# A bias row brought in by two transfers instead of a product, and two steps of a prologue in another order

## What is computed

```python
adj = dep_type_matrix != 0
dep_emb = dep_emb_table[dep_type_matrix]
hi_t = (h @ W1_w[:HID])[:, :, None, :] + dep_emb @ W1_w[HID:] + W1_b
hj_t = (h @ W2_w[:HID])[:, None, :, :] + dep_emb @ W2_w[HID:] + W2_b
relevance = jnp.sum(hi_t * hj_t, axis=-1)
A = jax.nn.softmax(jnp.where(adj, relevance, NEG), axis=2)
h_syn = jax.nn.relu((A @ h) @ gcn_w + gcn_b)
x = _layernorm(x + h_syn @ Wo_w + Wo_b)
```

## Time and profile before

| | us |
|---|---|
| median of 3 runs | 379.76 (379.12 to 379.9) |
| the profiled execution | 380.05 |
| its span, first to last instruction | 378.0 |
| TensorE busy | 372.1 (98%) |
| VectorE, ScalarE, GpSimd busy | 220.7, 142.1, 153.3 |

### The profile page before, as it was taken

One profiled execution on the slowest core, in us unless ns is written; L12 is line 12 of the kernel. 1 busy time (PEld: TensorE's weight loads), 2 busy tenths in 40 slices (PEclk: granted clock), 3 DMA queues, 4 the chain that ended last, 5 costly groups with the idle time before them and its releaser, 6 DMA issues.

```text
span 378.0 us, 10088 instructions
## 1 busy us (share of the span) xinstructions
PE 372.1 (98%) x4011; PEld 340.0 (90%) x4011; DVE 220.7 (58%) x584; ACT 142.1 (38%) x342; POOL 153.3 (41%) x133
## 2 busy tenths in 40 slices
PE   9999999999999999999999999999999999999994
PEld 4789898999989899998989989898998989999994
DVE  2546264674646567464666646476664646756596
ACT  1725442514334252333415234351423425142433
POOL 1333454270815418072450807236080632608035
PEclk9999999999999999999999999999999999999998
DMA  7922023508052260805317071441706245170105
GB/s 228 332 96 85 21 81 81 185 10 255 5 180 84 45 219 5 232 27 164 99 32 231 0 210 53 131 133 19 245 0 192 72 103 161 20 247 2 43 2 211
DMA packets 34851, 42.88 MB, mean 113 GB/s; under 512 B 10128, under 2 KB 29072, under 8 KB 34832
## 3 DMA queue, kind: packets, MB, share of 16 engines
q1 hardware_dynamic: 33600, 41.13, 36.3%
q10 hardware_dynamic: 1232, 1.49, 1.2%
HBM read 30.03 MB, written 12.58 MB: 113 GB/s over the span
## 4 chain that ended last, share of the span: by engine, by line
PE 98%; DVE 0%; POOL 0%; issue 0%
PE banks L447 18%; PE banks L449 18%; PE banks L448 18%; PE banks L547 9%; PE banks L548 9%; PE banks L553 9%; PE banks L526 7%; PE banks L471 7%; PE banks L571 2%; PE banks L560 1%; PE banks L506 1%; PE banks L581 0%; PE banks L597 0%; PE banks L592 0%; DVE xt_sb L1052 0%; PE banks L540 0%
## 5 line engine op out<-in xcount | busy, mean ns | idle before, releaser
L1160 POOL TENSOR_TENSOR x_sb<-x_sb,wob_sb 128x1536 f32<-128x1536 f32 x15 | 52.8, 3519 | 174.8 <-DVE weights L989 163.0
L958 DVE SCALAR_TENSOR_TENSOR hs_lo<-banks,hs_hi 128x256 fp32r<-128x256 f32 x90 | 32.6, 418 | 67.3 <-ACT hs_hi L818 67.2
L447 PE MATMUL banks<-gcn_hi,xt_hi 128*128 128x386 f32 x192 | 66.7, 347 | 0.0
L448 PE MATMUL banks<-gcn_lo,xt_hi 128*128 128x386 f32 x192 | 64.8, 338 | 0.0
L449 PE MATMUL banks<-gcn_hi,xt_lo 128*128 128x386 f32 x192 | 64.8, 337 | 0.0
L547 PE MATMUL banks<-wo_hi,hs_hi 128*128 128x384 f32 x180 | 60.9, 338 | 0.0
L553 PE MATMUL banks<-wo_hi,hs_lo 128*128 128x384 f32 x180 | 60.5, 336 | 0.0
L548 PE MATMUL banks<-wo_lo,hs_hi 128*128 128x384 f32 x180 | 60.5, 336 | 0.0
L759 ACT ACTIVATE gt_sb<-banks,r_sb 128x512 f32<-128x512 f32 x48 | 33.1, 689 | 70.2 <-PE banks L449 70.1
L447 PE MATMUL banks<-xt_hi,m_hi 128*128 128x512 f32 x144 | 57.4, 398 | 0.0
L449 PE MATMUL banks<-xt_hi,m_lo 128*128 128x512 f32 x144 | 56.8, 394 | 0.0
(11 more groups left out here) (101 smaller groups left out, 513.9 us busy)
## 6 DMA issues: line engine op xcount, KB each, us to landing
xt_sb<-in_x_t_dram SPq DMA_DIRECT2D x15, 768.0 KB, 4.6
x_sb<-in_x_dram SPq DMA_DIRECT2D x15, 768.0 KB, 5.6
out_dram<-y_sb SPq DMA_DIRECT2D x30, 384.0 KB, 5.8
adj_sb<-in_adj_dram SPq DMA_DIRECT2D x32, 64.0 KB, 2.3
xt_sb<-in_x_t_dram SPq DMA_DIRECT2D x2, 384.0 KB, 8.4
xt_sb<-in_x_dram SPq DMA_DIRECT2D x1, 768.0 KB, 4.9
w1t_sb<-in_w_t_dram ACTq DMA_DIRECT2D x3, 192.0 KB, 5.6
w2t_sb<-in_w_t_dram SPq DMA_DIRECT2D x3, 192.0 KB, 3.4
```

Source lines behind the costliest of these rows:

```text
L447: pe.matmul(acc, a_hi, b_hi, start=first, stop=False)
L448: pe.matmul(acc, a_hi, b_lo, start=False, stop=False)
L1160: pool.tensor_tensor(x_home(g, slot), x_home(g, slot), wob_sb[:].rearrange("p (o n) -> p o n", o=1).to_broadcast([P, PAIRS, HID]), ALU.add ...
```

## The change

The product of ones and `gb_diag` is gone, and with it `gb_diag`, its three VectorE instructions and the copy of `GB_BANK`. Instead ScalarE's queue writes gcn_b's three columns as one line of 384 numbers into device memory (`gb_line`), issued behind the biases and ahead of `w1t_sb[:, 1]`; behind gcn_w, ScalarE waits until that line has landed and issues a second transfer that repeats it in all 128 partitions of `gb_row`. On TensorE the third product of M's step 0 now stands behind the c products, and c2's share (L603, now L601) behind step 1 of M instead of ahead of it; step 1 waits for the first c2 result.

```diff
-        gb_diag = sb("gb_diag", [P, HID])
+        gb_line = nc.dram_tensor("gb_line", [1, HID], F32).ap()
...
-            def m_stage(c):
+            def m_stage(c, blocks=range(C)):
...
-                for d in range(C):
+                for d in blocks:
...
-            m_stage(0)
+            m_stage(0, range(C - 1))
...
             mm.then_inc(c_mm, 1)
-            pe.wait_ge(ones_ready, 1)
-            pe.wait_ge(gb_diag_ready, 1)
-            pe.matmul(GB_BANK[:, 0:HID], ones[:].to_broadcast([P, P]), gb_diag[:],
-                      start=True, stop=True).then_inc(gb_mm, 1)
+            m_stage(0, range(C - 1, C))
+            pe.wait_ge(c2_ready, 1)
+            m_stage(1)
             pe.wait_ge(c2_ready, 2)
...
-            m_stage(1)
             m_stage(2)
...
+            pe.wait_ge(ones_ready, 1)
...
-            pe.wait_ge(gb_row_ready, 1)
...
             act.dma_start(bias_sb[:], biases).then_inc(bias_loaded, 16)
+            act.dma_start(gb_line.rearrange("o (c p) -> o c p", p=P),
+                          biases[:, 2 * C:3 * C].rearrange("p (o c) -> o c p", o=1),
+                          allow_slow_non_contiguous=True).then_inc(gb_line_loaded, 16)
             for c in range(1, C):
                 act.dma_start(w1t_sb[:, c], w1_t[c * P:(c + 1) * P]).then_inc(w12_loaded[c], 16)
             for c in range(C):
                 act.dma_start(gcn_sb[:, c], gcn_w[c * P:(c + 1) * P]).then_inc(gcn_loaded[c], 16)
+            act.wait_ge(gb_line_loaded, 16)
+            act.dma_start(gb_row[:, 0:HID], gb_line.to_broadcast([P, HID])).then_inc(gb_row_spread, 16)
...
-                    dve.wait_ge(gb_row_ready, 1)
+                    dve.wait_ge(gb_row_spread, 16)
+                    dve.wait_ge(gb_end_zero, 1)
...
-            dve.memset(gb_row[:, HID:HID + 1], 0.0)
-            dve.wait_ge(ident_ready, 1)
-            for c in range(C):
-                a = dve.tensor_scalar(gb_diag[:, c * P:(c + 1) * P], ident[:], gb_sb[:, c:c + 1], None, ALU.mult)
-            a.then_inc(gb_diag_ready, 1)
+            dve.memset(gb_row[:, HID:HID + 1], 0.0).then_inc(gb_end_zero, 1)
...
-            dve.wait_ge(gb_mm, 1)
-            dve.tensor_copy(gb_row[:, 0:HID], GB_BANK[:, 0:HID]).then_inc(gb_row_ready, 1)
```

More of the change, by code:

```diff
@@ L176, in gnn_layernorm_kernel @@
         C_BANK = bank[3], bank[4]
-        GB_BANK = bank[2]
         ROWMAX_BANK = bank[4]
@@ L211, in gnn_layernorm_kernel @@
         c_mm = sem("c_mm")
-        gb_diag_ready = sem("gb_diag_ready")
-        gb_mm = sem("gb_mm")
-        gb_row_ready = sem("gb_row_ready")
+        gb_line_loaded = sem("gb_line_loaded")
+        gb_row_spread = sem("gb_row_spread")
+        gb_end_zero = sem("gb_end_zero")
         c12_sb_ready = sem("c12_sb_ready")
```

## The result

The changed kernel takes **399.45 us** in the median of 5 runs (397.07 to 400.79), before 379.76 (379.12 to 379.94 in 5 runs): a ratio of 1.052, with an interval of 1.048 to 1.056. It is 19.7 us slower. I had predicted 380.0, with a range to 384.6.

A forecast was written before the change was run, and what follows sets the result against it. TensorE, busy 98% of the span, was taken as the bound. 380.05 (profiled) - 0.84 + 1.05 (step 1 at 9.7 instead of 8.65) = 380.26; the profiled execution stands 0.29 over the median, so 380.0 us, range 378.8 to 384.6.

The forecast's parts named there:

- What bounds the kernel: Whole span: TensorE is busy for 98%; a microsecond off its prologue order brings everything behind it forward by a microsecond.
- What is removed: TensorE's prologue: dropping the gb_diag product at 8.65 us wins 0.84 us, if nothing else waits there.
- What is moved: TensorE's prologue: step 0's third product and c2's share cost the same in their new places, 0 us.
- The break-even of 9.49 for step 1: Start of M's step 1 on TensorE: later than 8.65 + 0.84 = 9.49 us makes the kernel slower.
- The line transfer: ScalarE's queue ahead of w1t_sb[:, 1]: 384 small packets delay those weights by 1.4 us, ends 0.26 and 7.3.
- The number of engines: In the line transfer's price: packets assumed spread over all 16 engines, 24 each; on three it would be 128 each.
- The slow rival: Line's packets on three engines, in turns with SyncE's: step 1 at 13.1, 383.4 us, in full 385.9; chance 0.27.
- The extra issue: ScalarE's queue: issuing the line takes about 0.45 us, counted as 0.2 us of delay to the weights' landing.
- The price of a packet into device memory: Line transfer: each 4-byte packet taken at 10.8 ns from ScalarE's early small packets, 57 ns when taking turns.
- The second transfer: ScalarE's wait for the line and load of gb_row: 0 us, line landing by 9.6 where 10.3 is allowed.
- The clock: In the slow rival: TensorE standing 4 us may fall back to its slower pace, 2.7 us at most on top.

The follow-up runs named there:

- order_only: The kernel before the change with TensorE's new order alone, the gb_diag product kept: 380.13 us against 380.10, ratio 0.9997.
- row_old_order: The changed kernel without the line transfer, gb_row loaded from a handed-over row of gcn_b, and TensorE's order of before: 379.48 us, ratio 0.9983 to before.
- line_16_sbuf: Against line_beside: the unused line's 384 numbers go into 128 on-chip partitions, partitions outermost, so sixteen engines: 380.28 us, ratio 1.002 to before.
- line_16_far: Against line_beside: partitions outermost, so sixteen engines, and each number written 512 bytes from the next in device memory: 379.97 us.
- line_sbuf: Against line_beside: same 3 by 128 pattern, but the unused line is written into one on-chip partition instead of device memory: 388.89 us.
- change_line_whole: The changed kernel with the line copied from a handed-over row, in 16 packets of 96 bytes instead of 384 of 4: 379.2 us, ratio 0.998 to before.
- line_beside: The changed kernel with gb_row loaded from a handed-over row of gcn_b; the line transfer stays in place, unused, waited for only at the end: 399.51 us.
- line_late: The changed kernel with the line transfer issued behind the three parts of gcn_w instead of ahead of w1t_sb[:, 1]: 405.33 us.
- line_quarter: Against line_beside: the unused line has 32 numbers of each of the three columns instead of 128: 386.91 us.

## Why the prediction was wrong, step by step

- **What bounds the kernel**: right. The 19 us are one wait of TensorE and what it did to the clock, and behind 34 us nothing differs.
- **What is removed, 0.84 us**: right in kind. row_direct, which has all of the change but the line, is 0.69 us under before in its median.
- **What is moved, 0**: right within 0.2 us (order_only, row_old_order).
- **The break-even of 9.49 for step 1**: right; the 16.5 us beyond it and the clock's 2.4 are the loss to a tenth.
- **The line transfer, 1.4 us**: this is the step that failed. Its ends were 0.26 and 7.3 us, and it came out at 17.9 us (landing at 25.9 instead of 8.0). Three things in it.
  - *The number of engines.* I chose sixteen because the bias load, the nearest row, uses them; but that load has the partitions outermost and the line has 3. The rule of the Trainium skill that the prediction names gave three, and the trace of after shows three completions. For sixteen engines 1.4 us was close (1.3 with the issue in it, in line_16_sbuf and line_16_far); for three the runs show 5.9 on the chip and 9.4 in device memory apart.
  - *The path behind the line.* The slow rival had the weights' parts on three engines stand behind the line, in turns with SyncE's packets. In line_sbuf no weights moved on any engine up to 9.5 us, and small packets went faster than turns allow. That its step 1 at 13.1 is near line_sbuf's 13.95 is therefore partly luck. Its 383.4 fell short of line_sbuf's 388.89 by the clock: 4.5 us of delay beyond the break-even and 4.6 of clock make the 9.0. The extra issue, put at 0.2, was 1.3 us long and moved the weights' issue by 1.4.
  - *The price of a packet into device memory.* The 10.8 ns were read off packets that go elsewhere. 128 neighbours of 4 bytes per engine delayed the weights by 131 ns each. No row of before writes device memory in small pieces, and I said so in the last sentence, but let 7.3 us stand as the upper end. An end without a row should have been left open and the range made wider.
- **The second transfer, 0**: right where the line is not slow (change_line_whole). In the change the line landed near 25.1 instead of by 9.6; that this cost nothing on top is only because the weights were as late (line_beside). In line_late it is the whole loss.
- **The clock**: named as a rival's addition, 2.7 us at most. It was 2.4 in the changed kernel's profiled execution, but 4.2 in line_beside, 4.4 in line_quarter and 4.6 in line_sbuf, where step 2 of M ran at the low clock as well. The bound was too low.

What stays open: why a whole queue stands behind packets on three engines, why neighbouring writes are that slow, and why SyncE's transfers and the issues stall with them. Between 12 and 15 us engines idle with work queued, but the trace does not say what holds it.

## What to carry to other kernels

Before a strided transfer goes into a queue, count its packets, see which dimension is outermost on both sides, and ask which loads stand behind it: three numbers in the outer dimension meant three engines, and the loads behind them on the same queue moved nothing on the other thirteen either (line_sbuf). Single numbers written side by side into device memory cost some twenty times the arithmetic that they replace here; a row that is whole already is repeated in all partitions at next to no cost. And where a price has no row in the trace, the upper end of the range is not the largest that the other rows give.

## What the runs showed of the hardware

- 4-byte writes into device memory side by side, on three engines: what stands behind them on their queue lands 4.0 us late for 32 per engine and 16.8 for 128 (125 and 131 ns each), and transfers of the other queue are held up as well. At 64 or 512 bytes apart the extra is gone with sixteen engines (step 1 with no wait, or at 9.43 us); with three, 512 bytes apart, 3.6 us over on-chip memory are left.
- 384 small packets on three engines into on-chip memory: the weights behind them land 5.9 us late, and their queue moves 0.00 MB from 5 to 9.5 us while the other queue fills all sixteen engines (line_sbuf). On sixteen engines it is 0.7 to 1.3 us.
- A transfer with 3 outermost took 1.3 us to issue, the same numbers with 128 outermost 0.46 to 0.66.
- The line behind gcn_w, with SyncE's queue still loading, took 30 us from issue to landing (line_late).
- After 16.7 us of standing TensorE's granted clock was 0.52 for the next 4.8 us of work, and in line_quarter, after a stand of 3.8 us, 0.51 for 8.9 us. A stand of 1.0 us (line_16_sbuf) left six passes at 2.18 us, where 3.8 us brought them to 4.19.
